# A two-layer field network on one core: three linear layers by a seven-product block scheme, activations kept unsplit

## The chip, the core and the metric

One core of a Trainium2 chip. The metric is the device time of the kernel in microseconds (us); three runs of the kernel before gave 595.06, 595.4 and 597.74 us, median 595.4.

## The reference, cut to what matters

For a batch of 512, eight embedding fields of 1024 numbers are gathered from eight tables (`iv[:, f]`). All arithmetic is float32.

```python
x_not = iv[:, [2, 3]]
t = tanh(relu(x_not @ Wn1 + bn1) @ Wn2 + bn2)        # Wn1, Wn2: 1024 x 1024
iv[:, [2, 3]] = t
def pair_fuse(pairs, W1, b1, W2, b2):                # W1: 2048 x 1024, W2: 1024 x 1024
    v = concatenate([iv[:, pairs[:, 0]], iv[:, pairs[:, 1]]], axis=-1)
    return relu(v @ W1 + b1) @ W2 + b2
s = pair_fuse([[0, 1], [2, 3]], Wa1, ba1, Wa2, ba2).sum(1) + pair_fuse([[4, 5]], Wo1, bo1, Wo2, bo2).sum(1)
z = (s + sum of the fields in no pair) / count
h = relu(concatenate([z, dense_ctx]) @ W_top1 + b_top1)
y = relu(h @ W_top2 + b_top2) @ W_top3               # 512 x 1
```

The indices of the fields are inputs: the kernel works with eight "slots" (two for NOT, four for the two AND pairs, two for the OR pair) whose fields it finds at run time.

## The kernel before

Activations lie transposed, a k-tile of 128 features by 512 batch columns. For float32 accuracy every operand of TensorE is split in two parts, hi and lo, and a product is three matmuls (hi x hi, hi x lo, lo x hi) of 128x128 by 128x512 into one PSUM bank. ScalarE writes the hi part (`split_hi`, L237), VectorE the lo part (`split_lo`, L409).

The work is twelve **units** of 1024x1024 by 512: Wn1 on two fields (units 0, 1), Wn2 on two fields (2, 3), the two halves of Wa1 on each of two pairs (4 to 7), the two halves of Wo1 (8, 9), Wa2 on the sum of both pairs' relu (10) and Wo2 (11). A unit is eight **pieces** (`unit`, L493), one per output tile; a piece is `product` (L479) with 8 k-tiles x 3 = 24 matmuls, all recorded at L485. Each piece uses one weight block of 512 KB, loaded by SyncE (L172) into one of two raw buffers when the block two before is split (SyncE waits on `w_lo`). After the units come the top layers: four more pieces, then 24 small matmuls (L576) and the last product (L583).

Slot 0's field is gathered in rows by POOL (L202), turned by TensorE (L507) and split to `X` (L260, L428). The other seven slots are gathered in quarter rows of 32 batch rows, 16 DMAs a slot (L209), through a ring of four staging buffers; VectorE turns each (`turn`, L398), and ScalarE and VectorE split it (L241, L404). Which unit fills which slot is in `UNIT_FILLS`. A unit's result is evacuated by ScalarE with bias and function in PSUM (L248), then split into hi (L250) and lo (L414). After the and units POOL gathers the sum of the fields in no pair into `V`, 8 accumulating gathers for each of 4 batch tiles, each waiting for the one before (L220); TensorE adds `V` into the output banks through the identity (L547) between units 10 and 11.

All engines run one instruction list each, in order, tied by counting semaphores; the order is written out by hand in the loops over units and pieces. PE's own order is `unit(0)` ... `unit(11)`, with a wait on `w_lo` for each piece and on `ev_lo` for the operand and the free bank.

## Time and profile before

| | |
|---|---|
| runs, median (lowest to highest) | 595.4 us (595.06 to 597.74) |
| profiled execution, span from first to last instruction | 594.9 us |
| what lies around the span, against the median | 0.5 us |
| TensorE busy | 578.7 us |
| VectorE, ScalarE, POOL busy | 292.8, 222.6, 164.7 us |
| read from HBM | 86.77 MB, 146 GB/s over the span |

The span is that of one profiled execution; no separate device time of it is given, so it is set beside the median of the three runs. Busy time is the time in which an engine executed; issuing a plain DMA and waiting on semaphores don't count. Windows give the same for a stretch, with PEclk, the granted TensorE clock as a share of full speed.

### The profile page before, as it was taken

To read this page: it belongs to the slowest core of one execution; us is meant where nothing else is said; L and a number is where in the kernel's file an instruction comes from. 1 tells how busy PE (TensorE), PEld (TensorE's weight loads), DVE (VectorE), ACT (ScalarE), POOL (GpSimd) and SP (SyncE) were. 2 spreads that over 40 slices of the span, in tenths; PEclk is the share of its full clock that TensorE was granted. 3 is DMA by queue.
4 is the path that set the end of the run, shared out by engine and by line. 5 is a ranking of instruction groups with operands and counts; after the bars stand their busy time and mean duration, and the time that the engine had idled before them with its cause. 6 is when DMAs were issued, how large, how long until landed. Compare 5 with 4: busy or idle time off the path is not lost.

```text
span 594.9 us, 8039 instructions
## 1 busy us (share of the span) xinstructions
PE 578.7 (97%) x2532; PEld 477.7 (80%) x2533; DVE 292.8 (49%) x465; ACT 222.6 (37%) x337; POOL 164.7 (28%) x152
## 2 busy tenths in 40 slices
PE   3999999999999999999999999999999997999998
PEld 3788888888888888888888888888888887988685
DVE  6866567666332765666223998652333121033321
ACT  2655555655344323332221444233343211044333
POOL 3433233333000533243001333466545440000000
PEclk9999999999999999999999999999999998999899
DMA  6544444444333544444233343569999996023300
GB/s 225 171 126 147 159 134 140 152 158 126 106 104 107 168 146 129 141 150 128 94 106 123 107 158 119 191 203 254 255 256 254 255 260 176 1 71 107 110 37 0
DMA packets 25767, 87.07 MB, mean 146 GB/s; under 512 B 4337, under 2 KB 4593, under 8 KB 25746
## 3 DMA queue, kind: packets, MB, share of 16 engines
q1 hardware_dynamic: 14754, 53.11, 27.0%
q0 software_dynamic: 10560, 33.56, 22.4%
q8 instruction: 13, 0.21, 0.2%
q10 hardware_dynamic: 432, 0.11, 0.1%
q14 instruction: 8, 0.07, 0.0%
HBM read 86.77 MB, written 0.00 MB: 146 GB/s over the span
## 4 chain that ended last, share of the span: by engine, by line
PE 78%; DMA 17%; DVE 2%; issue 1%; POOL 1%; ACT 0%; ACTq 0%; DVEq 0%; POOLq 0%
PE PS L485 74%; DMA V<-table,rows_rest 16%; PE PS L547 3%; PE PS L576 1%; POOL V L220 1%; DMA gathered<-identity 1%; PE PS L563 1%; DVE W L409 0%; PE PS L583 0%; POOL gathered L209 0%; DVE turned L347 0%; DVE gathered L351 0%; DVE X L404 0%; ACT V L298 0%; DVE turned L398 0%
## 5 line engine op out<-in xcount | busy, mean ns | idle before, releaser
L485 PE MATMUL PS<-X,W 128*128 (+1 forms) x2400 | 546.7, 390 | 1.3 <-DVE X L428 1.2
L485 PEld LDWEIGHTS PS<-X,W 128*128 128x128 f32 x2400 | 451.4, 188 | 96.4 <-DVE W L409 1.4
L209 POOL DMA_INDIRECT gathered<-table,rows x112 | 108.6, 970 | 275.6 <-DVE turned L398 253.8
L409 DVE TENSOR_TENSOR W<-w_raw,W 128x1024 fp32r<-128x1024 f32 x101 | 122.1, 1209 | 98.6 <-ACT W L237 89.0
L237 ACT ACTIVATE W<-w_raw 128x1024 fp32r<-128x1024 f32 x101 | 106.7, 1056 | 164.1 <-PE PS L485 131.9
L414 DVE TENSOR_TENSOR X<-PS,X (+1 forms) x52 | 36.0, 692 | 168.0 <-ACT X L250 168.0
L398 DVE STREAM_TRANSPOSE turned<-gathered 128x256 f32<-128x256 f32 x112 | 68.2, 647 | 1.2
L248 ACT ACTIVATE PS<-PS,col (+1 forms) x44 | 29.1, 662 | 105.1 <-PE PS L485 90.3
L220 POOL DMA_INDIRECT V<-table,rows_rest x32 | 51.8, 1618 | 42.2 <-DMA V<-table,rows_rest 40.7
L241 ACT ACTIVATE X<-turned 128x256 f32 (+1 forms) x112 | 45.1, 414 | 34.9 <-DVE turned L398 29.4
L404 DVE TENSOR_TENSOR X<-turned,X 128x256 f32 (+1 forms) x112 | 42.4, 420 | 0.1
L250 ACT ACTIVATE X<-PS (+1 forms) x52 | 31.1, 598 | 5.4
L248 ACT ACTIVATE PS<-PS,final_bias,inv x8 | 6.0, 750 | 44.2 <-PE PS L485 44.2
L547 PE MATMUL PS<-ident,V 128*128 128x128 f32 x64 | 15.5, 412 | 3.1 <-DMA V<-table,rows_rest 3.1
L547 PEld LDWEIGHTS PS<-ident,V 128*128 128x128 f32 x64 | 15.3, 335 | 3.4 <-issue 3.4
L507 PE MATMUL PS<-ident,V 128*128 128x128 f32 x32 | 5.8, 340 | 9.5 <-DMA V<-table,rows 9.5
L456 DVE TENSOR_SCALAR V<-PS,col x8 | 6.0, 751 | 14.9 <-PE PS L485 14.9
L507 PEld LDWEIGHTS PS<-ident,V 128*128 128x128 f32 x32 | 4.9, 203 | 9.9 <-issue 8.8
L463 DVE TENSOR_SCALAR PS<-PS,col 128x512 f32<-128x512 f32 x8 | 6.1, 759 | 5.5 <-PE PS L485 5.5
L260 ACT ACTIVATE X<-PS 128x512 fp32r<-128x512 f32 x8 | 4.0, 628 | 6.8 <-PE PS L507 6.8
L254 ACT ACTIVATE X<-V 128x512 fp32r<-128x512 f32 x8 | 4.9, 618 | 3.4 <-DVE V L466 3.4
L421 DVE TENSOR_TENSOR X<-V,X 128x512 fp32r<-128x512 f32 x8 | 5.5, 683 | 0.7 <-ACT X L254 0.7
(53 smaller groups left out, 45.7 us busy)
## 6 DMA issues: line engine op xcount, KB each, us to landing
w_raw<-weights SPq DMA_DIRECT2D x101, 512.0 KB
gathered<-table,rows POOLq DMA_INDIRECT x112
V<-table,rows_rest POOLq DMA_INDIRECT x32
gathered<-ints SPq DMA_DIRECT2D x1, 84.0 KB, 2.1
gathered<-identity ACTq DMA_DIRECT2D x1, 64.0 KB
V<-table,rows POOLq DMA_INDIRECT x4, 5.6
V<-dense_t SPq DMA_DIRECT2D x1, 32.0 KB, 3.3
V<-w_dense SPq DMA_DIRECT2D x1, 32.0 KB, 3.3
```

The source lines that it names most:

```text
L209: pool.indirect_dma_start(gathered[:, c % STAGE, :], None, table_quarters, bass.IndirectOffsetOnAxis(ap=rows[:, c // GROUPS, c % GROUPS:c ...
L220: pool.indirect_dma_start(Vf[:, H * b:H * (b + 1)], None, table, bass.IndirectOffsetOnAxis(ap=rows_rest[:, b, f:f + 1], axis=0), compute_o ...
L237: nc.scalar.activation(W_f[:, slot, 0, :], w_raw[:, slot, :], ACT.Copy).then_inc(w_hi, 1)
L241: nc.scalar.activation(X[:, SLOT_BUF[s], 0, :, bass.ds(g * 32, 32)], turned[:, e, :, :], ACT.Copy).then_inc(x_hi, 1)
L248: nc.scalar.activation(psum, psum, func, bias=bias, scale=scale).then_inc(full_out, 1)
L250: nc.scalar.activation(hi, psum, ACT.Copy).then_inc(ev_hi, 1)
L398: V_.transpose(turned[:, e, :, :], gathered[:, stage, :].rearrange("p (h k) -> p k h", k=KT))\
L404: V_.tensor_tensor(X[:, SLOT_BUF[s], 1, :, sl], turned[:, e, :, :], X[:, SLOT_BUF[s], 0, :, sl].bitcast(FP32), ALU.subtract).then_inc(x_lo, 1)
L409: V_.tensor_tensor(W_f[:, slot, 1, :], w_raw[:, slot, :], W_f[:, slot, 0, :].bitcast(FP32), ALU.subtract).then_inc(w_lo, 1)
L414: V_.tensor_tensor(X[:, buf, 1, bass.ds(tile, 1), :].rearrange("p o b -> p (o b)"), PS[:, bass.ds(bank, 1), :].rearrange("p o b -> p (o b) ...
L485: last = nc.tensor.matmul(PS[:, bank, :], w_of(slot, ws, k), x(xs, k), start=start and k == 0 and n == 0, stop=stop and k == k_tiles - 1 a ...
L547: last = nc.tensor.matmul(PS[:, m, P * b:P * (b + 1)], tile[:, m, :], ident[:, :].bitcast(FP32), start=False, stop=False)
```

## The change

Wn1, Wn2 and the two halves of Wa1 are no longer applied to two fields one after the other. The two fields side by side form one operand, cut in 2x2 blocks, and the product with a matrix in 2x2 blocks of 512x512 is made from seven block products (Strassen, in Winograd's order P1, P2, Q5, Q6, Q7, N4, Q3) in place of eight. A block product here is an **entry** of four **quarters**; a quarter is 4 k-tiles x 3 = 12 matmuls into one bank. Stages 0 and 1 (Wn1, Wn2) are seven entries each, stage 2 (both halves of Wa1 on both pairs) fourteen; the or layer and the second layers are eight entries of eight quarters, the top layer two of four. Entry e begins at quarter `FIRST[e]`: stage 1 at 28, stage 2 at 56, the or layer at 112, the A2/O2 entries at 144, the top layer at 176; the rest rows are added at 160.

The block scheme needs sums of operands. Sums of weights are made by accumulating DMAs that POOL issues (`add_quadrant`, 30 of 512 KB; Q5's two in stage 0 by VectorE). Sums of activations are called S1 to S4 and are POOL `tensor_tensor` of 128x1024 (30 of them; S1 of stage 0 by VectorE). Partial results are combined on chip in `XR` by VectorE (PSUM with SBUF) before ScalarE applies bias and function.

The split buffers of all activations `X` are gone. Raw activations stay in `XR` (8 buffers); the split operand `XO` holds two entries of 4 k-tiles, and each entry's operand is split, two k-tiles at a time, during the entry before it. Weights have seven raw slots instead of two. Fields are gathered by half slots (8 DMAs) without a ring, and a turn is two transposes of 128x1024 at a quarter named in `turn_at`. Weight loads come in quadrant pieces (2 blocks x 512 columns), 93 pieces for 101. The rest rows go to a buffer of `XR` in place of `V`.

The core of the diff: SyncE's loads.

```diff
-                    sp.dma_start(w_dense_sb, w_dense).then_inc(dense_in, 16)
+            def load(n):
+                slot = raw_slot(n)
+                sp.dma_start(raw_piece(slot), quadrant_rows(*block_rows(n))).then_inc(raw_in[slot], 16)
+
+            def load_after(n, split):
+
+                sp.wait_ge(w_lo, split + 1)
+                load(n)
+
+            load(0)
+            load(1)
+            load(2)
+            load(3)
+
+            for h in range(2):
+                sp.dma_start(raw_piece(2 + h), quadrant_rows(4 + 2 * h, 0)).then_inc(raw_in[2 + h], 16)
+            load(8)
+            for h in range(2):
+                sp.wait_ge(t1_sum, h + 1)
+                load(14 + h)
+            for n, split in ((9, 2), (12, 3), (13, 8), (16, 9), (28, 10), (29, 11), (17, 12), (22, 13), (23, 16),
+                             (26, 17), (27, 22), (32, 23), (30, 24), (31, 25), (33, 26), (34, 27), (35, 32), (44, 33),
+                             (45, 34), (46, 35), (47, 44), (52, 45), (53, 46), (54, 47), (56, 48), (57, 49), (58, 50),
+                             (59, 51), (55, 52)):
+                load_after(n, split)
+            for n in range(60, PIECES - 1):
```

POOL's list, from the start to the gathers of slots 6 and 7:

```diff
+            def add_quadrant(n, split):
+
+                e, h, slot = n // 2, n % 2, raw_slot(n)
+                kh, mh = ADDED[product_of(e)]
+                if split is None:
+                    pool.wait_ge(raw_in[slot], RAW_LOADED[n])
+                else:
+                    pool.wait_ge(w_lo, split + 1)
+                pool.dma_start(raw_piece(slot), quadrant_rows(8 * matrix_of(e) + 4 * mh + 2 * h, kh),
+                               accum_op=ALU.add).then_inc(w_sum[slot], 16)
+
+            def add_to(s, j, half=0):
+                e = entry_of(s, j, half)
+                before = None if j == Q7 else entry_of(s, {Q5: P1, Q6: Q5, N4: Q6}[j], half)
+                for h in range(2):
+                    add_quadrant(2 * e + h, None if before is None else 2 * before + h)
+
...
-                if c >= STAGE:
-
-                    pool.wait_ge(x_turned, c - STAGE + 1)
...
+            add_to(0, Q6)
+            pool.wait_ge(x0_raw, KT)
+            pool.wait_ge(s1_done, 2)
+            for kk in range(2):
+                G.tensor_tensor(XR[:, 1, 2 * kk:2 * kk + 2, :], XR[:, 1, 2 * kk:2 * kk + 2, :],
+                                XR[:, 0, 2 * kk:2 * kk + 2, :], ALU.subtract).then_inc(sums, 1)
+            for kk in range(2):
+                made(0, S3, 0, kk)
+                G.tensor_tensor(XR[:, 0, 2 * kk:2 * kk + 2, :], XR[:, 0, 2 * kk:2 * kk + 2, :],
+                                XR[:, 2, 4 + 2 * kk:6 + 2 * kk, :], ALU.subtract).then_inc(sums, 1)
+            add_to(0, Q7)
+            for kk in range(2):
+                made(0, S2, 0, kk)
+                G.tensor_tensor(XR[:, 0, 4 + 2 * kk:6 + 2 * kk, :], XR[:, 0, 4 + 2 * kk:6 + 2 * kk, :],
+                                XR[:, 0, 2 * kk:2 * kk + 2, :], ALU.subtract).then_inc(sums, 1)
+            add_to(0, N4)
+            for slot in (2, 3):
+                for h in range(2):
+                    gather_half(slot, h)
+
+
+            add_to(1, Q5)
+            pool.wait_ge(act_out, STAGE_OUT)
+            for kk in range(2):
+                G.tensor_tensor(XR[:, 1, 4 + 2 * kk:6 + 2 * kk, :], XR[:, 2, 2 * kk:2 * kk + 2, :],
+                                XR[:, 2, 4 + 2 * kk:6 + 2 * kk, :], ALU.subtract).then_inc(sums, 1)
+            for kk in range(2):
+                made(1, S1, 0, kk)
+                G.tensor_tensor(XR[:, 2, 2 * kk:2 * kk + 2, :], XR[:, 2, 2 * kk:2 * kk + 2, :],
+                                XR[:, 3, 2 * kk:2 * kk + 2, :], ALU.subtract).then_inc(sums, 1)
+            for kk in range(2):
+                made(1, S3, 0, kk)
+                pool.wait_ge(x_lo, x_done(entry_of(1, P1), kk))
+                G.tensor_tensor(XR[:, 3, 2 * kk:2 * kk + 2, :], XR[:, 3, 2 * kk:2 * kk + 2, :],
+                                XR[:, 1, 4 + 2 * kk:6 + 2 * kk, :], ALU.subtract).then_inc(sums, 1)
+            add_to(1, Q6)
+            for kk in range(2):
+                made(1, S2, 0, kk)
+                pool.wait_ge(x_lo, x_done(entry_of(1, P2), kk))
+                G.tensor_tensor(XR[:, 3, 4 + 2 * kk:6 + 2 * kk, :], XR[:, 3, 4 + 2 * kk:6 + 2 * kk, :],
+                                XR[:, 3, 2 * kk:2 * kk + 2, :], ALU.subtract).then_inc(sums, 1)
+            add_to(1, Q7)
+            for h in range(2):
+                gather_half(4, h)
+            add_to(1, N4)
+            made(1, S4, 0, 1)
+            pool.wait_ge(x_lo, x_done(entry_of(1, Q7), 1))
+            for h in range(2):
+                gather_half(5, h)
+
...
+            for half in range(2):
+                add_to(2, Q5, half)
+            pool.wait_ge(act_out, 2 * STAGE_OUT)
+            pool.wait_ge(turned, turned_count(5, 1))
+            for half in range(2):
+                pool.wait_ge(x_lo, x_done(entry_of(1, Q3), 1))
+                for kk in range(2):
+                    G.tensor_tensor(XR[:, 2 + half, 4 + 2 * kk:6 + 2 * kk, :], of_slot(4 + half, 2 * kk),
+                                    of_slot(4 + half, 4 + 2 * kk), ALU.subtract).then_inc(sums, 1)
...
+                                    XR[:, 4 + half, 2 * kk:2 * kk + 2, :], ALU.subtract).then_inc(sums, 1)
+            for j in (Q6, Q7, N4):
+                for half in range(2):
+                    add_to(2, j, half)
+
+
+            for slot in (6, 7):
+                for h in range(2):
+                    pool.wait_ge(x_lo, x_done(entry_of(2, N4, slot - 6), 1))
+                    if slot == 6:
+                        pool.wait_ge(x_lo, x_done(entry_of(2, Q6, h), 1))
+                        made(2, S4, h, 1)
+                    else:
+                        pool.wait_ge(turned, turned_count(6, h))
+                    gather_half(slot, h)
+
+            pool.wait_ge(turned, turned_count(7, 0))
+            pool.wait_ge(x_lo, x_done(entry_of(2, Q3, 0), 1))
             for f in range(F):
...
```

ScalarE: what a weight split waits for, and the evacuation of P1.

```diff
+            def split_w(n):
+                slot = raw_slot(n)
+                if n // 2 == entry_of(0, Q5):
+                    act.wait_ge(t1_sum, n % 2 + 1)
+                elif n in W_SUMMED:
+                    act.wait_ge(w_sum[slot], W_SUMMED[n])
+                else:
+                    act.wait_ge(raw_in[slot], RAW_LOADED[n])
+                if n >= 2:
+                    act.wait_ge(quarter, 2 * n - 2)
...
+                    if j == P1:
+                        act.wait_ge(quarter, t + 1)
+                        if s == 2 and m == 0:
+                            act.wait_ge(turned, turned_count(5, 1))
+                        nc.scalar.activation(place(s, "C21", m), PS[:, m, :], ACT.Copy).then_inc(e1_copied, 1)
...
```

VectorE's turn and its order by quarters t, and TensorE's loop:

```diff
+            def turn(slot, h):
+                dve.wait_ge(field_in[slot, h], 16 * 8)
+                of, to = staging(slot, h), SLOT_BUF[slot]
+                for i in range(2):
+                    b = 256 * h + 128 * i
+                    V_.transpose(XR[:, to, :, b:b + 128].rearrange("p k (g b) -> p g k b", b=32),
+                                 of[:, 1024 * i:1024 * (i + 1)].rearrange("p (g h k) -> p g k h", g=4, k=KT))\
+                        .then_inc(turned, 1)
...
+            turn_at = {28: (2, 0), 33: (2, 1), 37: (3, 0), 41: (3, 1), 50: (4, 0), 53: (4, 1), 60: (5, 0), 61: (5, 1),
+                       101: (6, 0), 105: (6, 1), 109: (7, 0), 113: (7, 1)}
+            for e in range(ENTRIES):
+                split_at = {1: (2, 3), 2: (2, 3), TOP - 1: (3, 5), TOP: (0, 1)}.get(e, (1, 2))
+                for m in range(QUARTERS_OF[e]):
+                    t = FIRST[e] + m
+                    if t:
+                        evacuate(t - 1)
+                    if t and t % 2 == 0:
+                        split_w(t // 2 + 1)
+                    for kk in range(2):
+                        if m == split_at[kk] and 2 <= e + 1 < ENTRIES:
+                            split_x(e + 1, kk)
...
+
+                        for h in range(2):
+                            dve.wait_ge(raw_in[2 + h], 16)
+                            V_.tensor_tensor(WR[:, h, :], WR[:, h, :], WR[:, 2 + h, :], ALU.add).then_inc(t1_sum, 1)
+                    if t in (3, 5):
+
+                        h = (t - 3) // 2
+                        turn(1, h)
+                        dve.wait_ge(turned, turned_count(1, h))
+                        V_.tensor_tensor(XR[:, 2, 4:8, 256 * h:256 * h + 256], XR[:, 1, 0:4, 256 * h:256 * h + 256],
+                                         XR[:, 1, 4:8, 256 * h:256 * h + 256], ALU.subtract).then_inc(s1_done, 1)
...
+                for m in range(4):
+                    t = FIRST[e] + m
+                    if t % 2 == 0:
+                        pe.wait_ge(w_lo, t // 2 + 1)
+                    if fresh:
+                        bank_free(m)
+                    elif half == 0:
+                        read_before(m)
+
+                    def x_there(k, e=e):
+                        if e < 2:
+                            pe.wait_ge(x_lo, 4 * e + k + 1)
+                        elif k % 2 == 0:
+                            pe.wait_ge(x_lo, x_done(e, k // 2))
+
+                    product(bank0 + m, t // 2 % 2, t % 2, x0, fresh, last_half(e),
+                            x_there if m == 0 else None)\
...
```

## Rows read from the trace of the kernel before

**Rows 1.** The page, busy time, share of the span and instructions of each engine
```profile
PE 578.7 (97%) x2532; PEld 477.7 (80%) x2533; DVE 292.8 (49%) x465; ACT 222.6 (37%) x337; POOL 164.7 (28%) x152
```

**Rows 2.** Groups by line and shape: busy us, mean ns | idle before, releaser
```profile
L485 PEld LDWEIGHTS PS<-X,W 128*128 128x128 f32 x2400 | 451.4, 188 | 96.4 <-DVE W L409 1.4 <-issue 1.3
L485 PE MATMUL PS<-X,W 128*128 x1536 | 348.6, 389 | 0.1
L485 PE MATMUL PS<-X,W 128*128 128x512 f32 x864 | 198.4, 392 | 1.2 <-DVE X L428 1.2
L409 DVE TENSOR_TENSOR W<-w_raw,W 128x1024 fp32r<-128x1024 f32 x101 | 122.1, 1209 | 98.6 <-ACT W L237 89.0 <-issue 9.3
L237 ACT ACTIVATE W<-w_raw 128x1024 fp32r<-128x1024 f32 x101 | 106.7, 1056 | 164.1 <-PE PS L485 131.9 <-DMA w_raw<-weights 32.1
L398 DVE STREAM_TRANSPOSE turned<-gathered 128x256 f32<-128x256 f32 x112 | 68.2, 647 | 1.2
L404 DVE TENSOR_TENSOR X<-turned,X 128x256 f32 x80 | 30.2, 420 | 0.0
L414 DVE TENSOR_TENSOR X<-PS,X x40 | 27.7, 692 | 135.9 <-ACT X L250 135.9
L248 ACT ACTIVATE PS<-PS,col x32 | 21.2, 662 | 74.2 <-PE PS L485 72.4 <-issue 1.8
L547 PE MATMUL PS<-ident,V 128*128 128x128 f32 x64 | 15.5, 412 | 3.1 <-DMA V<-table,rows_rest 3.1
...
L220 POOL DMA_INDIRECT V<-table,rows_rest x32: 937/1538/2567, 393.9 to 486.1; - x32
```

**Rows 3.** Window of units 0 to 7: us, PE busy (x), PEclk, DMA share, GB/s
```profile
16.59:365.02 348.43, 348.43 (x1536) 1.00 0.42 134
```

**Rows 4.** Windows around the rest rows on PE, and the chain of waits there
```profile
496.00:499.00 3.00, 0.00 (x0) 1.00 0.76 239
499.00:501.00 2.00, 1.98 (x8) 0.83 0.68 225
501.00:503.00 2.00, 2.00 (x11) 0.50 0.13 47
503.00:505.00 2.00, 2.00 (x10) 0.82 0.00 0
...
404.13 12.32 DMA V<-table,rows_rest
498.88 0.14 issue
499.02 15.51 PE PS L547 x64
```

**Rows 5.** Windows: PE, PEld, DVE, ACT, POOL busy (x), PEclk, DMA share, GB/s
```profile
393.90:498.90 105.00, 102.06 (x451) 84.17 (x449) 34.39 (x38) 30.97 (x41) 51.78 (x32) 1.00 1.03 256
...
5.00:10.00 5.00, 0.82 (x4) 0.85 (x5) 4.18 (x18) 2.11 (x2) 3.47 (x4) 1.00 0.87 289
```

**Rows 6.** Timeline of POOL: start, us, line, count [idle before]
```profile
17.09 0.95 POOL L209 DMA_INDIRECT gathered<-table,rows  x1 [0.30 <-issue]
18.34 0.95 POOL L209 DMA_INDIRECT gathered<-table,rows  x1 [0.30 <-issue]
...
402.13 1.55 POOL L220 DMA_INDIRECT V<-table,rows_rest  x1 [0.30 <-issue]
```

**Rows 7.** Start of the timeline; the x0 gathers (L202) and ints load to landing
```profile
4.37 1.10 POOL L202 DMA_INDIRECT V<-table,rows  x1 [3.92 <-DVE rows L330]
8.38 1.01 POOL L202 DMA_INDIRECT V<-table,rows  x1 [0.30 <-issue]
16.59 13.64 PE L485 MATMUL PS<-X,W 128*128 128x512 f32 x59 [1.22 <-DVE X L428]
...
DMA to landing us min/median/max: 4.7/5.6/5.9
...
gathered<-ints SPq DMA_DIRECT2D x1, 84.0 KB, 2.1
```

More of the change, by code:

```diff
@@ new lines, in operand_place, with out_place @@
+        def operand_place(s, j, half):
+            if s == 2:
+                return {Q5: (2 + half, 4), Q6: (4 + half, 0), Q7: (6 + half, 0), Q3: (4 + half, 4)}[j]
+            one, two, s1 = ((0, 1, (2, 4)) if s == 0 else (3, 2, (1, 4)))
+            return {P1: (one, 0), P2: (one, 4), Q5: s1, Q6: (one, 0), Q7: (two, 0), N4: (two, 4), Q3: (one, 4)}[j]
+        def out_place(s, which):
+            one, two = ((2, 3), (1, 0), (2, 3))[s]
+            return {"C11": (one, 0), "C12": (one, 4), "C21": (two, 0), "C22": (two, 4)}[which]
@@ L215, in _, with gather_half @@
-            pool.wait_ge(ev_lo, AND1_EV)
+            def gather_half(slot, h):
+                to = staging(slot, h)
+                for g in range(8):
+                    pool.indirect_dma_start(
+                        to[:, QC * g:QC * (g + 1)], None, table_quarters,
+                        bass.IndirectOffsetOnAxis(ap=rows[:, slot - 1, 8 * h + g:8 * h + g + 1], axis=0),
+                    ).then_inc(field_in[slot, h], 16)
+            def add_quadrant(n, split):
[7 more added lines that the diff above has]
+                               accum_op=ALU.add).then_inc(w_sum[slot], 16)
@@ new lines, in pair_sum @@
+            def pair_sum(t):
+                e = max(i for i in range(ENTRIES) if FIRST[i] <= t)
+                m = t - FIRST[e]
+                if e >= OZ or stage_of(e) != 2 or not last_half(e) or product_of(e) not in (N4, Q3):
+                    return
+                c, other, o = (("C11", "C21", C21_OUT) if product_of(e) == N4 else ("C12", "C22", C12_OUT))
+                dve.wait_ge(act_out, 2 * STAGE_OUT + o + m + 1)
+                V_.tensor_tensor(place(2, c, m), place(2, c, m), place(2, other, m), ALU.add).then_inc(pair_sums, 1)
@@ L477, in _, with product @@
+            evacuate(QUARTERS - 1)
         @block.tensor
         def _(pe):
-            def product(bank, slot, x, k_tiles, start, stop, w_of, before_k=None):
-                for k in range(k_tiles):
+            def product(bank, slot, i, x0, first, last, before_k=None):
+                for k in range(4):
                     if before_k is not None:
@@ L546, in _ @@
                     tile = Vf[:, H * b:H * (b + 1)].rearrange("p (c k) -> p k c", k=KT)
-                    last = nc.tensor.matmul(PS[:, m, P * b:P * (b + 1)], tile[:, m, :],
-                                            ident[:, :].bitcast(FP32), start=False, stop=False)
-            last.then_inc(rest_used, 1)
-            for j, t_buf in enumerate((T0_BUF, T1_BUF)):
-                weight = pe.value_load(tab[0:1, PAIR_SLOTS + j:PAIR_SLOTS + j + 1], min_val=0, max_val=1)
-                with pe.If(weight > 0):
-                    for m in range(KT):
-                        for xs in range(2):
-                            nc.tensor.matmul(PS[:, m, :], ident[:, :], X[:, t_buf, xs, m, :], start=False, stop=False)
@@ L564, in _ @@
[L564 to L571 removed]
+                pe.wait_ge(z_out, m + 1)
+                nc.tensor.matmul(PS[:, m, :], w_dense_sb[:, P * m:P * (m + 1)], dense_sb, start=True, stop=False,
+                                 skip_group_check=True)
@@ L589 @@
+            mm.then_inc(y_done, 1)
 def kernel(**inputs):
```

659 lines of the change are left out of this document (403 added, 256 removed).

## The prediction

> **What bounds the kernel now.** I read the page's busy times first, then the groups by shape, then windows and the chain. TensorE (PE) is busy 97% of a span of 594.9 us, VectorE (DVE) 49%, ScalarE (ACT) 37%, GpSimd (POOL) 28% [rows 1]. Nearly all of PE is one line, L485, 2400 matmuls with 1.3 us of idle time before them [rows 2]. Between 16.59 and 365.02 us PE issues 1536 of them without a gap, 348.43 / 1536 = 0.2268 us each [rows 3]; a "quarter" of 12 matmuls is 2.72 us. So a matmul taken out here is worth its full 0.227 us, as long as what feeds PE keeps up. In this chain only one wait stands, 3.06 us at 496 for the rest rows (L547) [rows 2, 4]. After it the granted clock is 0.50 between 501 and 503 and 0.83 and 0.82 in the two windows beside it [rows 4], that is 2 x (0.17 + 0.50 + 0.18) = 1.7 us lost (1.2 for 2.4 GHz). I charge every new wait of 3 us or more with this.
>
> **What is removed.** Units 0 to 7 are 8 x 192 = 1536 matmuls. The new order has 28 entries of 4 quarters, 28 x 48 = 1344. 192 x 0.2268 = **-43.6 us**. OR, the two second layers and the top layers keep their 768 + 96.
> The rest gather takes 105.0 us now, with the DMA engines full at 256 GB/s [rows 5], and ends 3.06 us late. In the new order it starts after the last half field is gathered and turned, about quarter 111.6, and is needed at quarter 160: 48.4 x 2.72 = 132 us. Even 20 us more would be hidden. So **-3.1 us** and -1.7 us of clock.
>
> **What is added, and what hides it.** DVE gets 93 weight splits for 101 (1.21 us each), 72 splits of two k-tiles (same shape, 1.21), 60 evacuations (0.69 each) and the same amount of transposing (68.2 us) [rows 2]: 112 + 87 + 41 + 68 and some 40 of small work is about 350 of 560 us. ACT: 93 x 1.056 + 72 x 1.056 + 60 x 0.66 is about 215 us. Neither is the bound on average. POOL gets 30 elementwise operations of 128x1024 and 30 accumulating DMAs. What decides is the order in each queue, since a late split stops PE. I go through the places with the least slack, in quarters (qN starts PE's quarter N).
>
> *Durations.* Split: ACT 1.06 then DVE 1.21, so 2.3 us. Transposing: 0.65 us for 256 columns, while a DVE operation of 256 takes 0.42 and one of 1024 takes 1.21 [rows 2], of which 0.16 is fixed; a turn is two of 128x1024, 2 x (0.16 + 4 x 0.49) = 4.2 us (at most 8 x 0.65 = 5.2). An indirect gather on POOL comes every 0.95 + 0.30 = 1.25 us, an accumulating one every 1.55 + 0.30 = 1.85 [rows 6]; I take 1.85 for the accumulating weight DMA. It lands 5.6 us after its issue, as the x0 gathers of the same 512 KB do [rows 7] (bounds 2.2, the small ints load [rows 7], and 12.3, a round of four rest gathers [rows 4]). **POOL's elementwise operation, g**, is in no row. Below: DVE's 1.21 for the same shape. Above: POOL's longest instruction, 2.57 [rows 2], plus one DVE operation in its way, 3.8. I take 2.5, by the POOL row. The Trainium skill (GPSIMD Engine Reference, Performance versus the Vector engine) measured 4497 ns for 2048 fp32, an estimate of 2.25 for 1024; the sum would come out about 1.5 us lower.
>
> *Start, +4 us (0 to 8.6).* SP now queues seven weight loads of 512 KB at once, before two. The x0 gathers are issued from 4.37 us and PE's first product starts at 16.59 [rows 7]; the engines move 289 GB/s then [rows 5]. 2.5 MB more cost 8.6 us if all of it goes first, half of that if the queues share. ACT's eight raw copies lie in its slack.
>
> *q8, +3.0 (2 to 5).* ACT is busy with 16 x0 copies until about 7.5 us after PE's start, so DVE's split of piece 2 ends at 9.9. Then turn and subtraction (4.2 + 0.2 + 1.2 = 5.6): 15.5; split: 16.7; second turn and subtraction: 22.3; the Q5 operand's split waits for it, ACT 23.4, DVE behind a weight split 24.7, for 8 x 2.72 = 21.8.
>
> *q12, +4.9 (0 to 10).* From q8: split 2.3, POOL's add DMA 1.85, S3 2g, S2 2g. With g = 2.5 the two halves of S2 are there at 11.65 and 14.15; ACT 12.7, 13.8, 15.2; DVE does operand, evacuation and weight split until 15.8, for 10.9.
>
> *q48, +8.0 (0 to 17).* N4's weights are the last link. From q36: split 2.3, add DMA 1.85, S4 2g = 5, two add DMAs for Q7 3.7, **16 gathers of field slot 4 at 1.25 = 20.0**, then N4's add DMA, landing 5.6, split 2.3: 40.7 us, for 12 x 2.72 = 32.7. The gathers stand ahead of a DMA that PE needs.
>
> *q56, +2.0.* From q50 DVE has evacuations, two weight splits, two operand splits and two turns before the split that q56 needs: 18.3 for 16.3. *q64, +4.0 (2 to 6).* Both halves of slot 5 are turned at q60 and q61, and ACT's evacuation of P1 waits for the second: 11.9 + 0.66 + 1.06 + 1.21 = 14.8 for 10.9.
>
> *q80, 0 (-0 to +19).* From q60: DVE 11.9, then 16 operations of g = 40, add DMA 5.6, split 2.3: 59.8, for 54.4 + 4.0 + 1.7 = 60.1. There is no slack left: each further us on g costs 16 us here.
>
> *Other transitions, 0.* The first product of a stage needs C21, which is out three quarters before; TOP's operand is split inside the last A2/O2 entry. If that cover went, it would be some 3 us each.
>
> *Clock.* Waits of 3 us or more are at q8, q12, q48, q64. Where the slow clock falls before the next late chain (after q8, after q48), it comes off that wait. It remains twice, +3.4 us.
>
> **Sum.** -43.6 - 3.1 - 1.7 + 4 + 3 + 4.9 + 8 + 2 + 4 + 0 + 3.4 = -19.1. On the profiled span of 594.9 that is 575.8; the median of the runs, 595.4, lies 0.5 above it, so I forecast **576 us**.
>
> **Rivals.**
> A. *The waits mostly don't come.* POOL's operations take DVE's 1.21, adds land sooner, the loads don't delay x0. Then q12 (4.9 and its clock 1.7), the start (4) and q48 (8) go: 576 - 18.6 = 557. For it: the DMA share is only 0.42 over the early stages [rows 3], so a lone add of 512 KB need not take what the crowded start shows. Against it: 20 us of gathers stand ahead of N4's add whatever g is, and nothing POOL does now is under 0.94.
> B. *POOL's chain becomes the bound of the and stage; slower than before.* Each operation on two on-chip inputs runs at 2.5 us and waits for a DVE operation of 1.21, g = 3.7. Then q12 gets 4 x 1.2 = 4.8; q48 gets 2.4, and 5.2 because S1, S3 and S2 (from 7.4 us after q28, six operations) end after q36's split instead of before it; q80 gets 16 x 1.2 = 19.2. 576 + 31.6 = 608. By the same arithmetic the gain is gone from g = 3.2. For it: DVE's operations with two on-chip inputs are four per entry pair, close to half of its time here. Against it: the present kernel has no POOL computation, so no row shows a collision. The Trainium skill (SBUF — State Buffer, Who interferes with whom) states it as a rule: a VectorE instruction with two SBUF inputs and a GpSimd instruction that reads SBUF share a port pair as an exclusive lock. By that rule the result is near B's time; no row of this profile can confirm or refute it.
> C. *The add DMAs are slow* (10 us instead of 5.6, toward the round of the rest): q48 and q80 get 4.4 each, and q12's weights 4 at most: 588.
>
> **How the numbers follow.** Forecast 0.50, its own range 567 to 587; A 0.22; B 0.20, of which a small part stops short of 592; C 0.08. A measurement tells about 0.5%, 3 us, from no change. Faster: 0.50 + 0.22 + 0.04 = 0.76. Same 0.06, slower 0.18, both out of B. The range goes to A's time and B's nearly: 555 to 606.
>
> **What would show it.** L485's successor has 2208 matmuls at 0.227 each and about 500 us. PE's waits lie at q8, q12, q48, q64 (DVE's or ACT's splits as the releaser), the largest at q48, released through a weight split whose ACT part waits for an accumulating DMA. The chain leaves PE for POOL there. L547's wait is gone. POOL's elementwise groups show near 2.5 us; at 3.2 or more, with DVE's 1.21 grown as well, B is right and the largest wait is at q80. Start of PE's first product near 20.6 us. The forecast is wrong in kind if PE's waits sum to under 10 us or over 45.

## The result, and the profile after it

| | before | changed |
|---|---|---|
| median of four runs, us | 596.56 | 631.56 |
| median without the slow runs, us | 596.56 | 625.97 |
| lowest and highest | 595.06, 597.74 | 621.45, 633.40 |
| profiled execution: span, us | 594.9 | 631.0 |
| TensorE's first product starts at, us | 16.59 | 21.16 |

Two of the four runs of the changed kernel (632.64 and 633.40) count as slow, so the ratios, the times and the differences of times given from here on are of fast runs alone, while the profiled execution, and with it the ledger below, is that of 632.64. The ratio is 1.049 with a 95% interval of 1.040 to 1.058. The change is **slower**, by 29 us (625.97 against 596.56), where I had forecast 19 us faster; every one of the four runs is also outside the range of 555 to 606.

The page of the changed kernel, busy times and costliest groups. Line 840 is the successor of 485, 683 of 409 (VectorE's weight split), 527 of 237 (ScalarE's), 739 and 556 split operands, 381 is the accumulating DMA on weights, 464 to 481 are the sums of stage 2. These answer to [rows 1, 2].

```profile
PE 553.2 (88%) x2340; PEld 448.5 (71%) x2340; DVE 398.2 (63%) x350; ACT 225.3 (36%) x261; POOL 309.6 (49%) x212
...
L840 PE MATMUL PS<-XO,WO 128*128 128x512 f32 x2208 | 520.8, 397 | 61.9 <-DVE WO L683 41.5
...
L683 DVE TENSOR_TENSOR WO<-WR,WO 128x1024 fp32r<-128x1024 f32 x93 | 159.4, 1715 | 171.5 <-ACT WO L527 171.3
L527 ACT ACTIVATE WO<-WR 128x1024 fp32r<-128x1024 f32 x93 | 98.5, 1059 | 297.9 <-PE PS L840 248.7
...
L739 DVE TENSOR_TENSOR XO<-XR,XO 128x1024 fp32r<-128x1024 f32 x64 | 100.0, 1564 | 0.9 <-ACT XO L556 0.7
...
L746 DVE STREAM_TRANSPOSE XR<-XR 128x1024 f32<-128x1024 f32 x28 | 58.2, 2119 | 0.0
L770 DVE TENSOR_TENSOR XR<-PS,XR 128x512 f32<-128x512 f32 x48 | 32.5, 687 | 19.3 <-PE PS L840 19.3
...
L469 POOL TENSOR_TENSOR XR<-XR 128x1024 f32 x4 | 13.4, 3377 | 0.0
```

The ledger closes. TensorE's product line was busy 547.0 us and waited 1.3 (its two shapes together, [rows 2]); now it is busy 520.8 and waits 61.9. At 0.2268 us the 2208 matmuls are 500.8, so 20.0 us are time at a lower clock (before, 547.0 for 2400 x 0.2268 = 544.3, so 2.7). Change of the span: busy -26.2, waits +60.6, first product +4.6, the rest rows' wait -3.1, together +35.9, for 631.0 - 594.9 = +36.1. The 43.6 us of the forecast did come off; the slower clock took 17.3 of them back, and the waits outweigh the rest. What failed is the feed.

Two things are to be seen on VectorE. ScalarE's weight split is as it was (1059 ns, before 1056), and so are VectorE's evacuations, which read one operand from PSUM (687 ns, before 692), and its transposes, which read one tile (2119 ns, never far from it). But its subtractions of two on-chip tiles went from 1209 ns to 1715 and 1564.

Where TensorE waited 4 us or more: its timeline; in brackets the idle time before the row and what ended it.

```profile
71.36 1.19 PE L840 MATMUL PS<-XO,WO 128*128 128x512 f32 x2 [12.11 <-DVE XO L739]
...
141.51 2.07 PE L840 MATMUL PS<-XO,WO 128*128 128x512 f32 x4 [13.73 <-DVE WO L683]
...
170.53 2.03 PE L840 MATMUL PS<-XO,WO 128*128 128x512 f32 x4 [4.55 <-DVE WO L683]
...
200.08 1.22 PE L840 MATMUL PS<-XO,WO 128*128 128x512 f32 x2 [5.90 <-DVE WO L683]
...
253.62 2.92 PE L840 MATMUL PS<-XO,WO 128*128 128x512 f32 x6 [4.53 <-DVE WO L683]
...
311.11 1.22 PE L840 MATMUL PS<-XO,WO 128*128 128x512 f32 x2 [4.35 <-DVE WO L683]
```

By the matmuls issued before each (144, 384, 480, 576, 768 and 960, 12 to a quarter) these are q12, q32, q40, q48, q64 and q80. The two longest have their reason beside them, in VectorE's and GpSimd's timelines of the same stretches. VectorE first:

```profile
53.85 0.69 DVE L770 TENSOR_TENSOR XR<-PS,XR 128x512 f32<-128x512 f32 x1 [2.03 <-PE PS L840]
55.00 15.07 DVE L683 TENSOR_TENSOR WO<-WR,WO 128x1024 fp32r<-128x1024 f32 x1 [0.46 <-ACT WO L527]
70.00 1.21 DVE L739 TENSOR_TENSOR XO<-XR,XO 128x1024 fp32r<-128x1024 f32 x1
...
123.31 1.18 DVE L739 TENSOR_TENSOR XO<-XR,XO 128x1024 fp32r<-128x1024 f32 x1
124.42 17.03 DVE L683 TENSOR_TENSOR WO<-WR,WO 128x1024 fp32r<-128x1024 f32 x1
```

GpSimd (xN: so many in a row, the time is that of all):

```profile
51.23 1.22 POOL L381 DMA_DIRECT2D WR<-weights  x1 [2.71 <-DVE WO L683]
52.10 5.22 POOL L405 TENSOR_TENSOR XR<-XR 128x1024 f32<-128x1024 f32 x2
56.81 5.13 POOL L409 TENSOR_TENSOR XR<-XR 128x1024 f32<-128x1024 f32 x2
61.45 2.87 POOL L381 DMA_DIRECT2D WR<-weights  x2
62.93 6.05 POOL L414 TENSOR_TENSOR XR<-XR 128x1024 f32<-128x1024 f32 x2
...
123.87 2.62 POOL L381 DMA_DIRECT2D WR<-weights  x2
125.43 5.76 POOL L425 TENSOR_TENSOR XR<-XR 128x1024 f32<-128x1024 f32 x2
130.11 5.67 POOL L429 TENSOR_TENSOR XR<-XR 128x1024 f32<-128x1024 f32 x2
134.70 5.66 POOL L434 TENSOR_TENSOR XR<-XR 128x1024 f32<-128x1024 f32 x2
```

One subtraction of 1.2 us on VectorE lasts 15 and 17 us, until GpSimd's six sums are through (68.98 and 140.36). ScalarE's timeline shows that both long waits of TensorE hang on it, and not on a sum or a weight that came late:

```profile
59.74 1.06 ACT L556 ACTIVATE XO<-XR 128x1024 fp32r<-128x1024 f32 x1 [4.77 <-POOL XR L409]
...
122.43 1.07 ACT L527 ACTIVATE WO<-WR 128x1024 fp32r<-128x1024 f32 x1 [2.18 <-PE PS L840]
```

At q12 the hi part of the operand is there at 60.80, and VectorE begins its lo part at 70.00, behind the held weight split. At q32 the hi part of the weight is there at 123.50, and the lo part is the held subtraction itself. Two sums start 56.81 - 52.10 = 4.71 us apart, 2.35 each. In stage 2 the two engines take turns instead: each VectorE subtraction lasts 3.4 us and one GpSimd sum ends in each of them (four at 3377 ns on line 469). VectorE there:

```profile
276.82 3.42 DVE L683 TENSOR_TENSOR WO<-WR,WO 128x1024 fp32r<-128x1024 f32 x1
280.15 3.40 DVE L739 TENSOR_TENSOR XO<-XR,XO 128x1024 fp32r<-128x1024 f32 x1
283.48 3.41 DVE L683 TENSOR_TENSOR WO<-WR,WO 128x1024 fp32r<-128x1024 f32 x1
```

The clock, in windows over the two long waits (TensorE busy, TensorE weight loads, VectorE, ScalarE, GpSimd, then the granted clock, DMA share, GB/s); compare [rows 4]:

```profile
60.00:70.00 10.00, 0.00 (x0) 0.00 (x0) 10.00 (x2) 3.75 (x4) 8.98 (x5) 0.57 0.62 103
70.00:80.00 10.00, 8.64 (x30) 7.04 (x31) 7.19 (x9) 1.09 (x2) 5.30 (x5) 0.75 0.71 104
130.00:140.00 10.00, 0.00 (x0) 0.00 (x0) 10.00 (x1) 0.36 (x1) 10.00 (x5) 0.65 0.21 39
140.00:150.00 10.00, 8.49 (x27) 6.80 (x28) 8.85 (x6) 0.94 (x2) 0.36 (x1) 0.66 0.37 105
```

TensorE idles through a window, and the clock is still down while it works again in the next.

### The profile page after: what moved, and what is told of

It reads as the page before. It is cut to its first block, busy times and chain, and to the rows that moved or that the text cites. A ratio compares the mean times of both kernels' runs of the same rounds, so it can differ in the third digit from the quotient of the medians.

```text
span 631.0 us, 5966 instructions
## 1 busy us (share of the span) xinstructions
PE 553.2 (88%) x2340; PEld 448.5 (71%) x2340; DVE 398.2 (63%) x350; ACT 225.3 (36%) x261; POOL 309.6 (49%) x212
## 4 chain that ended last, share of the span: by engine, by line
PE 38%; issue 9%; DVE 8%; DMA 8%; POOL 2%; ACT 1%; POOLq 0%; DVEq 0%; ACTq 0%
PE PS L840 33%; DMA WR<-weights 8%; DVE XR L746 3%; DVE WO L683 2%; PE PS L937 2%; POOL XR L481 2%; DVE XO L739 1%; ACT WO L527 1%; PE PS L957 1%; DVE XR L770 1%; PE PS L945 1%; DVE XR L788 1%; PE PS L964 0%; ACT XR L623 0%; ACT XR L626 0%
## 5 line engine op out<-in xcount | busy, mean ns | idle before, releaser
L840 PE MATMUL PS<-XO,WO 128*128 128x512 f32 x2208 | 520.8, 397 | 61.9 <-DVE WO L683 41.5
L840 PEld LDWEIGHTS PS<-XO,WO 128*128 128x128 f32 x2208 | 421.9, 192 | 160.8 <-DVE WO L683 47.9
L683 DVE TENSOR_TENSOR WO<-WR,WO 128x1024 fp32r<-128x1024 f32 x93 | 159.4, 1715 | 171.5 <-ACT WO L527 171.3
L527 ACT ACTIVATE WO<-WR 128x1024 fp32r<-128x1024 f32 x93 | 98.5, 1059 | 297.9 <-PE PS L840 248.7
L368 POOL DMA_INDIRECT XR<-table,rows x112 | 130.5, 1165 | 46.0 <-issue 33.8
L739 DVE TENSOR_TENSOR XO<-XR,XO 128x1024 fp32r<-128x1024 f32 x64 | 100.0, 1564 | 0.9 <-ACT XO L556 0.7
L381 POOL DMA_DIRECT2D WR<-weights x30 | 37.9, 1867 | 87.3 <-DVE WO L683 62.0
L556 ACT ACTIVATE XO<-XR 128x1024 fp32r<-128x1024 f32 (+1 forms) x72 | 75.1, 1045 | 11.3 <-POOL XR L409 6.0
L504 POOL DMA_INDIRECT XR<-table,rows_rest x32 | 52.0, 1625 | 40.1 <-DMA XR<-table,rows_rest 38.3
L746 DVE STREAM_TRANSPOSE XR<-XR 128x1024 f32<-128x1024 f32 x28 | 58.2, 2119 | 0.0
L866 PE MATMUL PS<-ident,XR 128*128 128x128 f32 x32 | 6.4, 362 | 13.5 <-DMA XR<-table,rows 13.5
L469 POOL TENSOR_TENSOR XR<-XR 128x1024 f32 x4 | 13.4, 3377 | 0.0
L475 POOL TENSOR_TENSOR XR<-XR 128x1024 f32<-128x1024 f32 x4 | 13.4, 3374 | 0.0
L481 POOL TENSOR_TENSOR XR<-XR 128x1024 f32<-128x1024 f32 x4 | 13.4, 3375 | 0.0
```

The lines of the kernel that those rows point to most:

```text
L368: pool.indirect_dma_start(to[:, QC * g:QC * (g + 1)], None, table_quarters, bass.IndirectOffsetOnAxis(ap=rows[:, slot - 1, 8 * h + g:8 * h ...
L381: pool.dma_start(raw_piece(slot), quadrant_rows(8 * matrix_of(e) + 4 * mh + 2 * h, kh), accum_op=ALU.add).then_inc(w_sum[slot], 16)
L481: G.tensor_tensor(XR[:, 4 + half, 4 + 2 * kk:6 + 2 * kk, :], of_slot(2 + half, 4 + 2 * kk), XR[:, 4 + half, 2 * kk:2 * kk + 2, :], ALU.sub ...
L504: pool.indirect_dma_start(Vf[:, H * b:H * (b + 1)], None, table, bass.IndirectOffsetOnAxis(ap=rows_rest[:, b, f:f + 1], axis=0), compute_o ...
L527: nc.scalar.activation(WO[:, n % 2, 0, :], WR[:, slot, :], ACT.Copy).then_inc(w_hi, 1)
L556: nc.scalar.activation(XO[:, s1:s1 + 2, 0, :], source(e, kk, regs), ACT.Copy, scale=scale)\
```

## The experiments

There were three theories. **Contention**: GpSimd's sums and VectorE's two-tile subtractions keep each other out. **Queue**: GpSimd's queue is in a bad order (gathers ahead of a DMA that TensorE needs). **VectorE full**: its order and load would make these waits anyway. The waits of TensorE and its slow clock below are taken as in the ledger above, each from one profiled execution; medians and ratios are of the timed runs.

### The sums on one column

The operand sums do one column of 512; the rest of them is left out.

```diff
-G.tensor_tensor(XR[:, 1, 2 * kk:2 * kk + 2, :], XR[:, 1, 2 * kk:2 * kk + 2, :],
-                XR[:, 0, 2 * kk:2 * kk + 2, :], ALU.subtract)
+G.tensor_tensor(XR[:, 1, 2 * kk:2 * kk + 2, 0:1], XR[:, 1, 2 * kk:2 * kk + 2, 0:1],
+                XR[:, 0, 2 * kk:2 * kk + 2, 0:1], ALU.subtract)
 ...
```

> POOL's 30 subtractions are cut to one column of each k-tile (2 numbers per partition instead of 1024); the rest of the sums is left out. Everything else, all waits included, stays. Theory P (POOL's operations hold a port that VectorE's two-input operations need): VectorE's weight split is back at 1.21 us mean (from 1.72), none over 1.3; the waits at q12 and at the start of stage 1 (12.1 and 13.7 us) and the slow stretch in stage 2 go; about 590 us, between 582 and 600. Theory Q (the order of POOL's queue, DMA issue and landing, is what costs): only the 30 x 2.3 us of POOL time go, VectorE's longest operations stay, time over 612 us. Theory D (VectorE is overfull with turns): over 618 us.

Measured: 588.7 us, ratio 0.984 (0.979 to 0.988): 37 us less than with the sums, and 42.9 between the two profiled executions. In the groups by line:

```profile
L840 PE MATMUL PS<-XO,WO 128*128 128x512 f32 x2208 | 513.6, 395 | 27.0 <-DVE WO L683 19.6 <-issue 5.3 <-DVE XO L739 2.0
...
L683 DVE TENSOR_TENSOR WO<-WR,WO 128x1024 fp32r<-128x1024 f32 x93 | 113.9, 1226 | 191.4 <-ACT WO L527 181.3 <-issue 10.1
```

VectorE's split is back at 1226 ns, the two long waits are gone, waits fall by 34.9 and slow clock by 7.2 (to 12.8). The sums are the main cost; this kernel takes away both their time on GpSimd and their hold on VectorE, and does not tell the two apart. What is left has its largest wait, 9.76 us, at q48: N4's weight DMAs are issued at 160.63 behind 16 gathers that begin at 134.36, 1.64 us each where I had taken 1.25.

### Each sum waits for the one before it to end

```diff
+if n_sums[0]:
+    pool.wait_ge(sums, n_sums[0])
+n_sums[0] += 1
 nc.gpsimd.tensor_tensor(out, one, two, ALU.subtract).then_inc(sums, 1)
```

> Each of POOL's 30 subtractions waits for the end of the one before it, nothing else is changed; results as in the changed kernel. Theory P with starvation (a chain queued back to back never lets VectorE in, a gap does): VectorE's longest weight split falls from 17.0 us to 3.5 or less, PE's two waits of 12.1 and 13.7 us shrink to 2 to 6 each, about 610 us (603 to 618). Theory P without the part on gaps: the longest stays over 10 us and the time at 625 to 635. Theory Q: 631 or up to 3 us more.

Measured: 629.0 us, ratio 1.052 (1.045 to 1.058), where the theory with gaps had said 603 to 618. The long holds went (VectorE's longest subtraction 5.9 us, mean of the weight split 1444 ns), but TensorE still waits 54.0 us, and runs 25.1 us of slow clock. So the 15 and 17 us holds are not the cost by themselves: what VectorE gets back, GpSimd loses, and its sums come later.

### N4's weight DMAs ahead of the gathers

```diff
 add_to(1, Q7)
+add_to(1, N4)
 for h in range(2):
     gather_half(4, h)
-add_to(1, N4)
```

> Stage 1's accumulating weight DMAs for N4 are issued ahead of the 16 gathers of slot 4. Theory Q: PE's wait of 5.9 us at q48 goes with its slow clock, and what stands behind moves up; 10 us or more gained. Theory P: that wait goes too, but it is the only one that does: 5 to 8 us gained, and slot 4's turn may come late by as much as 2.7 us.

Measured: 638.4 us, ratio 1.066 (1.060 to 1.071). The wait at q48 is gone, as expected, and the time is 10 to 12 us longer (by the ratios, by the medians), where both theories had said shorter. Later waits took its place (5.4 us at q104), so the waits fall by only 2.6, to 59.3, but the slow clock costs 28.5 for 20.0. Why it costs more with fewer waits stays open.

The same move where the sums are on one column (left out as above):

> e1 (POOL's subtractions on one column, the rest of the sums left out) with N4's weight add ahead of slot 4's gathers. In e1 PE waits 9.8 us at q48, for an add issued 26 us after its turn came, behind 16 gathers. If that order alone is the cause, the wait goes with its slow clock: 10 to 13 us under e1, so 577 to 580 us. If the add is slow by itself, 589 as e1.

Measured: 578.7 us against 588.7 (two runs and three); waits 15.7, slow clock 12.2. The order of GpSimd's queue is worth about 10 us, as the expectation had it, but only once its sums are out of the way.

### Unused sums in the kernel before

Twelve unused 128x1024 subtractions on GpSimd in the fourth stage, the first six each waiting for the last but one (as below), the others each for the one before.

```diff
+for i in range(6):
+    if i >= 2:
+        pool.wait_ge(burst, i - 1)
+    nc.gpsimd.tensor_tensor(V[:, 2 * (i % 2):2 * (i % 2) + 2, :], V[:, 4:6, :], V[:, 6:8, :], ALU.subtract).then_inc(burst, 1)
```

> The kernel before, with 12 idle POOL subtractions of 128x1024 on the unused buffer V during unit 3: six queued back to back (each waits for the one two before it), then, four pieces later, six of which each waits for the end of the one before. Their results are not used. Theory P: in the first burst VectorE's weight split (two on-chip inputs) lasts until the burst ends, 8 to 14 us, and PE waits 5 to 10 us; in the second no weight split is over 3.5 us; the lo part of an evacuation, which reads PSUM, and transposes stay at 0.69 and 0.65. Time 5 to 13 us over before. Theories Q and D: no VectorE operation changes, time as before within 1 us.

Measured: 597.63 us, ratio 1.001 (0.999 to 1.003). VectorE at the first train:

```profile
155.45 3.39 DVE L421 TENSOR_TENSOR W<-w_raw,W 128x1024 fp32r<-128x1024 f32 x1
160.26 0.69 DVE L426 TENSOR_TENSOR X<-PS,X  x1 [1.42 <-ACT X L262]
160.94 1.24 DVE L421 TENSOR_TENSOR W<-w_raw,W 128x1024 fp32r<-128x1024 f32 x1
```

The 3.4 us appear in the kernel before too, on the subtraction of two SBUF tiles and not on the evacuation from PSUM; there is room for them there, and the 5 to 13 us that the first theory had expected do not come. No hold of 15 us. The next kernel has the same train in place, and a second that stands right behind an accumulating DMA of GpSimd's own:

```diff
+pool.dma_start(V[:, 6:8, :].rearrange("p k b -> p (k b)"),
+               weights[0:1, :, :].rearrange("o p c -> p (o c)"), accum_op=ALU.add).then_inc(burst_dma, 16)
+for i in range(6):
+    pool.wait_ge(burst, 5 + i)
+    a = V[:, 2 * (i % 2):2 * (i % 2) + 2, :]
+    nc.gpsimd.tensor_tensor(a, a, V[:, 4:6, :], ALU.subtract).then_inc(burst, 1)
```

> The kernel before with two other bursts of six POOL subtractions in unit 3. First: in place (a = a - c), each waiting for the one two before it. Second: the same, each waiting for the one before it, directly behind an accumulating weight DMA that POOL issues. In e4 a VectorE weight split waited for one POOL operation at most (3.4 us); in the changed kernel for six in a row (15 and 17 us). If operations in place are what keeps VectorE out, the first burst holds a split for over 8 us; if the DMA issued just ahead is, the second does; if neither, both stay at 3.5 us.

Measured in a single run (611.48 us): the first train takes turns again (3.39 at most). The second, GpSimd and then VectorE:

```profile
169.87 0.96 POOL L216 DMA_DIRECT2D V<-weights  x1 [1.29 <-PE PS L504]
170.52 14.27 POOL L222 TENSOR_TENSOR V<-V 128x1024 f32<-128x1024 f32 x6
```

```profile
172.16 13.72 DVE L428 TENSOR_TENSOR W<-w_raw,W 128x1024 fp32r<-128x1024 f32 x1
185.81 0.68 DVE L433 TENSOR_TENSOR X<-PS,X  x1
```

A hold of 13.7 us, for all six sums, though each waits for the end of the one before. The next asks what makes it: a train that waits until its DMA has landed, one with a single SBUF operand, and one as the second above.

```diff
+if j == 0:
+    pool.wait_ge(burst_dma, 16)
 ...
+if j == 1:
+    nc.gpsimd.tensor_scalar(a, a, 0.5, None, ALU.mult).then_inc(burst, 1)
+else:
+    nc.gpsimd.tensor_tensor(a, a, V[:, 4:6, :], ALU.subtract).then_inc(burst, 1)
```

> The kernel before with three trains of six unused 128x1024 GpSimd operations in its fourth stage, each operation started by the end of the one before, and each train led by an accumulating DMA from GpSimd's queue: the first train waits until the DMA has landed, the second has one SBUF operand (a multiplication by a constant), the third is the two-operand subtraction directly behind the DMA. If what keeps VectorE out is the DMA still open while GpSimd runs two-operand operations, then the first train lets VectorE's weight splits through at 3.0 to 3.6 us each (alternating, as in the trains without a DMA), and the third holds one for 12 to 15 us. If the hold comes from the DMA instruction itself, whenever it landed, the first train holds one for 12 to 15 us too. If it is the port alone that counts, the one-operand train holds nothing (splits of 1.2 us), and otherwise it holds one as the third does.

Measured in a single run (612.12 us), VectorE beside the first, second and third train:

```profile
171.42 2.21 DVE L429 TENSOR_TENSOR W<-w_raw,W 128x1024 fp32r<-128x1024 f32 x1
...
182.30 1.23 DVE L429 TENSOR_TENSOR W<-w_raw,W 128x1024 fp32r<-128x1024 f32 x1
...
195.39 5.81 DVE L424 TENSOR_TENSOR X<-turned,X 128x256 f32 x2
```

With the DMA landed no hold (2.21 at most), with one operand hardly any delay (2.51 once, then 1.23, though a multiplication was running). But the third train made none either: 5.81 for two short operations is one turn of some 2.5 us lost before each. It was there to show the hold again, so the first train alone says nothing of what the landing does. A DMA issued just ahead stands ahead of every hold of over 13 us (two in the changed kernel, two in the one with N4's DMAs first, two in the last kernel below, one in the kernel with the trains in place), and does not suffice for one: the kernel in which each sum waits for the one before has the same DMAs ahead of its sums, and 5.9 us at most.

### The sums wait for the landing

In four places (Q6 and Q7 of stage 0, Q5 and Q6 of stage 1) GpSimd waits until the DMA that it has just issued has landed.

```diff
+def landed(s, j):
+    n = 2 * entry_of(s, j) + 1
+    pool.wait_ge(w_sum[raw_slot(n)], W_SUMMED[n])
 ...
 add_to(0, Q6)
+landed(0, Q6)
```

> The changed kernel, where GpSimd waits for the landing of the accumulating DMA that it has just issued before it begins a group of sums (four places, in stages 0 and 1). If the hold needs an open DMA, VectorE's longest weight split falls from 17.0 us to under 5, the two long waits of TensorE (12.1 and 13.7 us) shrink to under 6 each, against it stand four landings of some 6 us in GpSimd's queue, which bring back some 3 to 6 us at the sums' own deadlines: 612 to 625 us, against 631.6. If the hold does not need an open DMA, the splits of 15 to 17 us stay, and the time is 632 to 642.

Measured: 643.1 us, ratio 1.077 (1.072 to 1.083). The first theory's half on VectorE came (no subtraction over 3.42 us), its half on the time did not: 643 for 612 to 625. GpSimd starts stage 1's sums at 143.07 for 125.43, the wait at q12 is still 8.9 us (12.1 before), and TensorE's wait of 13.7 us at q32 is now one of 16.3 at q36 (432 matmuls before it), where the operand made from the first of these sums is due:

```profile
154.48 2.07 PE L848 MATMUL PS<-XO,WO 128*128 128x512 f32 x4 [16.34 <-DVE WO L691]
```

ScalarE's operand splits idle 16.6 us for these sums in its groups. So the holds are one face of the cost, and sums that come late are the other: taking one away brings out the other. No run has the sums at GpSimd's own pace without VectorE beside them, so how much of the time belongs to each is not shown.

### All sums on VectorE

The 30 subtractions move into VectorE's order, ahead of their use; N4's DMAs stand ahead of the gathers; slot 5's second half gets a staging place of its own; the transposes are spread.

```diff
-G.tensor_tensor(XR[:, 1, 2 * kk:2 * kk + 2, :], XR[:, 1, 2 * kk:2 * kk + 2, :],
-                XR[:, 0, 2 * kk:2 * kk + 2, :], ALU.subtract).then_inc(sums, 1)
 ...
+V_.tensor_tensor(to, x, y, ALU.subtract).then_inc(sums, 1)
```

> The 30 subtractions of activations move from POOL to VectorE (1.2 us each there), and with them: N4's weight add ahead of slot 4's gathers, slot 5's second half staged in another buffer so that P1's evacuation needn't wait for its turn, and the turns spread over other quarters. Results as in the changed kernel. Theory P (a POOL operation costs VectorE 2.2 us of waiting in stage 2 and up to 15 in stages 0 and 1, more than the 1.2 us of doing it itself): no VectorE operation over 1.4 us but transposes, PE's waits at most 25 us in sum, 575 to 590 us, under the kernel before. Theory D (VectorE is overfull; its list has about 128 of 133 us from quarter 28 to 77 in it): the waits only change place and sum to 40 us or more, 600 us or over.

Measured: 594.7 us, ratio 0.996 (0.993 to 1.000): over the 575 to 590 of the first theory, and under the 600 of the third. The weight split is at 1226 ns again, waits 27.7, of which 15.8 have no releaser (the profile shows nothing that was waited for). Then SP also waits for the last gathered x0 rows before it loads piece 2:

```diff
 load(1)
+sp.wait_ge(x0_in[BT - 1], 16)
 load(2)
```

> e5, and SyncE holds back all weight loads but the first two until slot 0's rows are there. If the loads delay the x0 gathers by sharing the DMA engines, PE's first product starts at 16.5 to 17.5 us instead of 21.2 and the time is 3 to 4 us under e5. Rival: what comes next (pieces 2 and 3, the two addends of Q5) is then late by as much, and the time stays within 1 us of e5.

Measured: 588.9 us, ratio 0.984 (0.979 to 0.989). The first product starts at 16.9 us, for 21.25 with the seven loads at once; whether the time gains the 3 to 4 us expected is not told by runs that reach from 582.94 to 596.66. Last, the transposes one by one instead of in pairs:

```diff
-turn_at = {23: (2, 0), 27: (2, 1),
+turn_at = {23: (2, 0, 0), 25: (2, 0, 1), 27: (2, 1, 0), 29: (2, 1, 1),
 ...
```

> The version with all sums on VectorE, weight sums ahead of the gathers and the late first loads, now with the 24 transposes of 128x1024 put one by one into VectorE's order, two quarters apart, instead of in pairs of 4.1 us. The theory that what is left there is VectorE's order (a weight split behind two transposes, 5.7 us at 339 us) says that this wait falls under 3 us and the time by 3 to 6 us, to about 588 to 591 us. The rival, that VectorE is simply full in these stages, says 592 to 596.

Measured: **571.6 us** (569.10 to 572.46), ratio 0.958 (0.954 to 0.962), against 588 to 591 by the better theory. In the groups by line:

```profile
L825 PE MATMUL PS<-XO,WO 128*128 128x512 f32 x2208 | 506.2, 391 | 17.0 <-DVE WO L622 14.1 <-DVE XO L678 1.6 <-ACT XR L542 1.3
...
L622 DVE TENSOR_TENSOR WO<-WR,WO 128x1024 fp32r<-128x1024 f32 x93 | 113.5, 1221 | 148.8 <-ACT WO L466 140.9 <-issue 7.9
```

No wait of over 2 us is left behind q4; the version before had 5.7 at 339 us, behind two transposes in a row. At q4 one of 7.4 stands. It is not from the later loads: ScalarE splits the weight for it at 33.01, and at 25.86 in the next kernel, which has the same loads, and idles 5.57 us before 28.67 without a releaser.

The gain is larger than expected because a stretch of stalls at 173 to 195 us is gone as well. The version before showed it without a releaser and with the clock at 0.51 to 1.00 from one window to the next:

```profile
179.80 6.54 PE L825 MATMUL PS<-XO,WO 128*128 128x512 f32 x17 [6.59 <-issue]
```

ScalarE idles there too, 8.70 us before 188.75, without a releaser. Why such stalls come and go between kernels, no run tells. They are not in the changed kernel and not in the next, and they blur what each step above was worth.

### The same, with the sums left on GpSimd

```diff
 load(1)
+sp.wait_ge(x0_in[BT - 1], 16)
 load(2)
 ...
+add_to(1, N4)
 for h in range(2):
     gather_half(4, h)
-add_to(1, N4)
 ...
-turn_at = {28: (2, 0), 33: (2, 1),
+turn_at = {28: (2, 0, 0), 30: (2, 0, 1), 33: (2, 1, 0), 35: (2, 1, 1),
 ...
```

> The changed kernel with its sums left on GpSimd, but with what the last version has beside them: N4's weight sums ahead of the gathers of the fifth slot, first loads behind the gathered rows, and 22 of its 24 transposes set one by one, two quarters apart (those of the sixth slot stay in pairs). If the sums' engine is what separates 572.3 from 631.6 us, VectorE's splits are still held (one of 13 to 17 us in each of stages 0 and 1, and 3.4 us each in stage 2) and the time is 605 to 632 us. If it is the order of loads, gathers and transposes, the time is 575 to 595 us though the splits are held.

Twenty of the 24 transposes of 128x1024 stand one by one here; the four of slot 5 stay in pairs. Measured: 611.9 us, ratio 1.027 (1.023 to 1.030). VectorE's timeline and group:

```profile
52.33 13.60 DVE L684 TENSOR_TENSOR WO<-WR,WO 128x1024 fp32r<-128x1024 f32 x1 [0.46 <-ACT WO L528]
125.27 14.29 DVE L684 TENSOR_TENSOR WO<-WR,WO 128x1024 fp32r<-128x1024 f32 x1 [1.01 <-ACT WO L528]
```

```profile
L684 DVE TENSOR_TENSOR WO<-WR,WO 128x1024 fp32r<-128x1024 f32 x93 | 155.0, 1668 | 156.9 <-ACT WO L528 156.9
```

So of the 54 us between the change (626.0) and the version before this one (571.6), 14 belong to the order of loads, gathers and transposes, and 40 to the move of the sums with the placing that goes with it. The kernel with nearly empty sums says 37 for the same thing from the other side.

## Why the prediction was wrong

- **-43.6 for 192 matmuls, -3.1 and -1.7 for the rest rows: right.** 2208 at 0.2268 us, and the wait is gone.
- **Start, +4: right**, +4.6, and the cause too: with the loads held back the first product is at 16.5 to 16.9.
- **g = 2.5: the step that failed, in what it was taken to be.** The sum charges it to GpSimd's chain alone and puts its effect on VectorE's splits at nothing. As the sum's own length it was close: 2.35 back to back (14.27 / 6 = 2.38 in the second train). When the engines take turns a sum comes every 3.34 us (276.82 to 280.15 on VectorE), and makes a subtraction of VectorE 3.4 us for 1.2. On GpSimd a sum costs VectorE 2.2 us, more than the 1.2 it would take there.
- **q12, +4.9: 12.1. q32 and q40, not in the sum at all: 13.7 and 4.5.** The chain that I had counted for q12 was right: both halves of S2 are there at 61.94, 13.9 us after q8 began, for 14.15. The rest of the wait is the held weight split, behind which VectorE's part of the operand stands. I looked at slack where an operand or a weight had a long chain. At q32 the weight split has none: it was only in VectorE's queue while GpSimd did its sums. The whole of TensorE's waits, 61.9 us, is over the 45 above which I had called the forecast wrong in kind, and the largest is at q32, not at q48.
- **q48, +8.0: 5.9, and 9.8 without the sums.** The mechanism, 16 gathers ahead of a DMA that TensorE needs, is shown by its removal. **q56, +2.0: 2.0. q64, +4.0: 4.5.** These two follow from VectorE's order alone, and counting it worked. q8: 2.2 for 3.0.
- **q80, 0 (up to +19): 4.3**, and 1.0, 1.7 and 1.7 at three quarters ahead of it, 8.7 in all. My formula gives 16 x (3.34 - 2.5) = 13.4.
- **Clock, +3.4: 20.0** in the product line. I had charged 1.7 for each of two waits. There are two waits of over 12 us, and eight of 1.7 to 5.9. The loss grows with the waits, but only roughly: waits of 17.0, 27.0, 44.8 and 61.9 us in all go with 5.4, 12.8, 19.7 and 20.0, and 15.7, 54.0 and 59.3 with 12.2, 25.1 and 28.5. So no price for one wait comes out of these runs.
- **The rivals.** B had the right side and the right mechanism, and I gave it 0.20. (My chances also did not add up: same and slower make 0.24 "both out of B", which has 0.20, and C's 588 is faster than no change.) Its condition was met (3.34 us for a sum beside VectorE, over the break-even of 3.2), its place was not: it puts the cost at q80 and into GpSimd's chain (608), while most came through VectorE's splits in stages 0 and 1, and in the clock. Its sentence from the Trainium skill (SBUF — State Buffer, Who interferes with whom) says that two SBUF operands on VectorE and a GpSimd instruction that reads SBUF exclude each other. For the sums the trace agrees: 3.4 us for 1.2, with evacuations from PSUM (687 ns) and transposes (2119) untouched. For a multiplication with one SBUF operand it does not: beside it two of three subtractions took 1.23 us. What I should have done with it is what the sum lacked: apply the exclusion to VectorE's splits at each place of GpSimd's sums, not only to the sums. A did not occur; C's slow DMA did in part (median landing 7.7 us for 5.6), under the rest.
